# A four-layer graph network on one core: the second head's up-projection placed in steps around the first head's softmax

## The chip, the cores and the metric

One NeuronCore of one Trainium2 chip runs the kernel. The metric is the device time of one execution in microseconds (us), less is better. The engines are named by what they do here: TensorE (PE in the rows) multiplies, VectorE (DVE), ScalarE (ACT) and GpSimd (POOL) do the elementwise work, and SyncE (SP) issues most weight loads.

## What is computed

The input is `x` (256 nodes, 768 features) with 8192 edges (src, dst, and a type for layer 3). Four layers each add a graph part and a feed-forward part to `x`, each on a layer-normed input. The change touches layers 0 and 1, whose graph part is a two-stage graph attention:

```
def gat_conv(x, src, dst, W, a_src, a_dst, b, heads, out_ch):
    h = (x @ W).reshape(n, heads, out_ch)              # up-projection, 768 -> 8 heads x 768
    e = leaky_relu(alpha_src[src] + alpha_dst[dst], 0.2)
    p = exp(e - segment_max(e, dst)[dst])
    alpha = p / segment_sum(p, dst)[dst]
    out = segment_sum(h[src] * alpha, dst)             # attend
    return out.reshape(n, heads * out_ch) + b

h = elu(gat_conv(x, ..., W1, 8 heads, 768))            # 8 hidden heads
out = gat_conv(h, ..., W2, 1 head, 768)                # down-projection 8*768 -> 768, then attend again
```

Then come small feed-forward parts, a GCN layer (2) and a relational GCN layer with 34 relations (3), which the change leaves alone.

## The kernel before

The engines run programs of their own, ordered by hand and tied by semaphores; no planner is involved. All edges are first counted into dense 256x256 matrices (`cnt`), so that the segment softmax becomes a row softmax over a dense matrix weighted with the counts, and `attend` becomes a matmul with its transpose. The counting (`count`, 16 batches of 4 tiles of edges) shares the start of the kernel with head 0 of layer 0: VectorE and ScalarE make one-hot and ramp tiles in a ring of three, and TensorE takes them in between the steps of head 0's up-projection.

All weights stream through SBUF in chunks of 768x768 (six 128-row tiles, two parts of three). SP loads a part into `w_in` (`load`); ScalarE rounds it to the high half `w_hi` (`high`), and VectorE makes the rest `w_lo` (`low`). Each product of two values is three fp32r matmuls, high x high, high x low and low x high (`mm3`). Both `w_hi` and `w_lo` have two halves, so that one chunk is used while the next is made. `w_in` has one place for each part, so that a load waits until the part before it is rounded and its rest made.

A hidden head `h` is worked so, with one chunk of W1 and one of W2:

- TensorE: `up` (12 steps: 2 node tiles m times 6 tiles k, each two outputs of 384 columns, 6 matmuls), then `down(h - 1)` in three pieces (of its 12 steps 3, 6 and 3), with `spread(h)` (the source scores laid out as a row in bank 7) after 3 and `turn(h)` (the transpose of `alpha`) after 9, then `attend(h)` (36 matmuls of 256 columns, in three groups).
- ScalarE: keeps `h_sb` and `h_hi` from the banks (`keep_tile`), exponentials of the scores, `aT_hi`, then `z_b` (`kept`), the exponential for elu (`exponential`) and the rounding of `hid_hi` (`rounded`), and the high halves of two weight chunks in between.
- VectorE: four dot products for the scores (the third releases `spread`), softmax in `scores` to `alpha` (semaphore `normed`), a low part `ahead`, `aT_lo`, a second low part, then elu (`negative`, `unit`), `batch_firsts` (which edge of a cell is its first, for a table on layer 3's relations), `remainder` (`hid_lo`), and the low parts of the W2 chunk.

Head 0 has no `down` before it. Between its `spread`, `turn` and `attend` TensorE runs zero matmuls (`seed`, `idle`: 128x128 zeros with 512 columns), 3 of which also clear the sums in banks 0, 1 and 2. The heads 1 to 7 are one loop on TensorE; ScalarE and VectorE have head 0 and head 7 written out. The last head does the three elu stages interleaved, the others stage after stage. The chunk of a W1 sits in half `layer` of the weight buffers, that of a W2 in half `1 - layer`.

SP starts with the load of chunk 1, then waits until it has arrived, clears the 9 MB `table` in HBM, and goes on with the loads W1(1), W2(0), W1(2), W2(1) and so on. GpSimd adds the edges into that table with indirect DMAs.

`step_of`, `up`, `down`, `attend`, `spread`, `turn`, `seed` and `idle` are TensorE's functions; the helper line 435 records nearly all its matmuls, line 531 the transposes of `alpha`. ScalarE's helper `keep` is line 948, VectorE's `tt` is 1267 and `dot` 1273.

## Time and profile before

| | us |
|---|---|
| median of 3 runs | 1368.61 (1365.76 to 1372.85) |
| the profiled execution | 1376.49 |
| its span, first to last instruction | 1374.5 |
| TensorE matmuls busy | 1304.2 (95%) |
| VectorE busy | 994.7 (72%) |
| ScalarE busy | 646.9 (47%) |
| share of TensorE in the chain that ended last | 82% |
| mean granted TensorE clock | 0.98 |

A granted clock of 1.00 is 2.4 GHz, 0.50 is 1.2 GHz. Times in the rows are us from the span's start. A row of a timeline stands for one or several like instructions in a row; its second number runs from the first start to the last end.

### The profile page before, as it was taken

How to read it: one execution, taken by the hardware profiler on the slowest of the kernel's cores; microseconds unless marked ns; L12 is line 12 of the kernel's file. 1: busy time of each engine (PE TensorE's matmuls, PEld its weight loads, DVE VectorE, ACT ScalarE, POOL GpSimd, SP SyncE). 2: the span in 40 equal slices, each digit the busy share in tenths (PEclk: the TensorE clock that was granted, in tenths of full speed). 3: DMA queues.
4: the chain of work that ended last, by engine and by line, in shares of the span. 5: the costliest groups of instructions: out<-in, count | busy, mean ns of one | idle time of the engine just before them, and what ended most of it. 6: DMA issues, size and time to landing. Idle time of an engine off the chain costs nothing.

```text
span 1374.5 us, 21211 instructions
## 1 busy us (share of the span) xinstructions
PE 1304.2 (95%) x7822; PEld 1153.0 (84%) x7822; DVE 994.7 (72%) x1634; ACT 646.9 (47%) x845; POOL 215.7 (16%) x160
## 2 busy tenths in 40 slices
PE   6899999988899999988898999999999999999987
PEld 5699999965799999967777888988898888988876
DVE  7888888987688888876757666655666556665556
ACT  5666565554466565654334343333433344333342
POOL 0034443340034444440000000000000000002000
PEclk9999999999999999998989999999999999999989
DMA  9755665654355665635314644554445444553530
GB/s 306 262 177 168 179 212 181 196 130 136 107 175 168 197 205 175 193 92 178 108 60 167 223 153 154 188 190 154 153 164 192 178 153 153 177 194 117 179 91 28
DMA packets 103875, 227.33 MB, mean 165 GB/s; under 512 B 16710, under 2 KB 34950, under 8 KB 103840
## 3 DMA queue, kind: packets, MB, share of 16 engines
q1 hardware_dynamic: 72924, 192.43, 40.0%
q10 hardware_dynamic: 20980, 31.78, 8.2%
q0 software_dynamic: 9936, 2.66, 2.0%
q8 instruction: 21, 0.34, 0.1%
q14 instruction: 14, 0.11, 0.0%
HBM read 216.56 MB, written 10.29 MB: 165 GB/s over the span
## 4 chain that ended last, share of the span: by engine, by line
PE 82%; DVE 11%; ACT 2%; issue 2%; DMA 1%; ACTq 0%; DVEq 0%; SPq 0%
PE bank L435 81%; DVE w_lo L1267 3%; DVE stats L1305 1%; ACT w_hi L948 1%; PE bank L474 1%; DVE h_lo L1267 1%; PE bank L531 1%; DMA w_in<-L_gnn_W_root 1%; DVE xT_lo L1267 1%; DVE neg_b L1270 0%; DMA x_sb<-x 0%; DVE x_sb L1267 0%; DMA w_in<-L_gnn_W 0%; DVE scores_b L1273 0%; DVE hid_lo L1267 0%
## 5 line engine op out<-in xcount | busy, mean ns | idle before, releaser
L1267 DVE TENSOR_TENSOR w_lo<-w_in,w_hi 128x2304 fp32r<-128x2304 f32 (+4 forms) x162 | 396.5, 2477 | 60.7 <-ACT w_hi L948 60.6
L948 ACT ACTIVATE w_hi<-w_in 128x2304 fp32r<-128x2304 f32 (+4 forms) x162 | 328.1, 2062 | 224.3 <-PE bank L435 197.2
L435 PE MATMUL bank<-w_hi,xT_hi 128*128 128x384 f32 (+3 forms) x942 | 326.3, 346 | 4.7 <-DVE xT_lo L1267 3.4
L435 PE MATMUL bank<-w_lo,xT_hi 128*128 128x384 f32 (+3 forms) x942 | 309.8, 341 | 0.0
L435 PE MATMUL bank<-w_hi,hid_hi 128*128 128x512 f32 (+3 forms) x858 | 293.5, 342 | 5.0 <-DVE hid_lo L1267 4.8
L435 PE MATMUL bank<-w_lo,hid_hi 128*128 128x512 f32 (+3 forms) x858 | 271.7, 337 | 0.0
L435 PE MATMUL bank<-w_hi,xT_lo 128*128 128x384 f32 (+3 forms) x942 | 247.5, 341 | 0.0
L435 PE MATMUL bank<-w_hi,hid_lo 128*128 128x512 f32 (+3 forms) x858 | 224.9, 338 | 0.0
L435 PEld LDWEIGHTS bank<-w_hi,xT_hi 128*128 128x128 f32 (+1 forms) x942 | 178.9, 190 | 31.9 <-issue 6.2
L435 PEld LDWEIGHTS bank<-w_hi,hid_hi 128*128 128x128 f32 (+1 forms) x858 | 161.5, 188 | 41.2 <-issue 5.9
L435 PEld LDWEIGHTS bank<-w_lo,xT_hi 128*128 128x128 f32 (+1 forms) x942 | 179.0, 190 | 13.2
L1774 DVE SCALAR_TENSOR_TENSOR neg_b<-bank,rinv,neg_b 128x512 f32<-128x512 f32 (+1 forms) x136 | 77.5, 611 | 154.4 <-PE bank L435 154.4
L435 PEld LDWEIGHTS bank<-w_lo,hid_hi 128*128 128x128 f32 (+1 forms) x858 | 161.7, 188 | 18.4
L394 POOL DMA_INDIRECT table<-value,row_i x64 | 122.8, 1919 | 243.0 <-DMA table<-value,row_i 224.7
L435 PEld LDWEIGHTS bank<-w_hi,xT_lo 128*128 128x128 f32 (+1 forms) x942 | 157.9, 191 | 2.1
L435 PEld LDWEIGHTS bank<-w_hi,hid_lo 128*128 128x128 f32 (+1 forms) x858 | 134.5, 190 | 1.0
L435 PE MATMUL bank<-aT_hi,h_hi 128*128 128x256 f32 (+1 forms) x408 | 107.5, 283 | 2.2 <-DVE aT_lo L1267 2.2
L435 PE MATMUL bank<-aT_hi,h_lo 128*128 128x256 f32 (+1 forms) x408 | 107.6, 286 | 0.0
L948 ACT ACTIVATE xT_hi<-bank 128x512 fp32r<-128x512 f32 (+1 forms) x87 | 46.8, 554 | 124.9 <-PE bank L435 63.5
L435 PE MATMUL bank<-aT_lo,h_hi 128*128 128x256 f32 x396 | 104.8, 283 | 0.0
L420 POOL DMA_INDIRECT w_in<-L_gnn_W_rel,xrow_i x6 | 7.3, 1216 | 527.1 <-DVE w_lo L1267 525.6
L435 PEld LDWEIGHTS bank<-aT_hi,h_hi 128*128 128x128 f32 x408 | 78.3, 192 | 5.0 <-DVE aT_lo L1267 3.6
(252 smaller groups left out, 1566.2 us busy)
## 6 DMA issues: line engine op xcount, KB each, us to landing
w_in<-L_gnn_W_rel SPq DMA_DIRECT2D x68, 1152.0 KB, 5.9
w_in<-L_gnn_W SPq DMA_DIRECT2D x66, 1152.0 KB, 6.2
table<-zrow SPq DMA_DIRECT2D x1, 9216.0 KB, 31.6
scores_b<-table ACTq DMA_DIRECT2D x34, 256.0 KB, 3.0
a_bc<-L_gnn_a_src ACTq DMA_DIRECT2D x18, 384.0 KB, 3.8
a_bc<-L_gnn_a_dst ACTq DMA_DIRECT2D x18, 384.0 KB, 5.3
key_row<-key_rows ACTq DMA_DIRECT2D x16, 256.0 KB, 5.4
w_in<-ffn_out SPq DMA_DIRECT2D x4, 864.0 KB, 7.3
```

Of the source, the lines that this page charges most:

```text
L394: pool.indirect_dma_start(out=cells, out_offset=bass.IndirectOffsetOnAxis(ap=row_i[:, g:g + 1], axis=0), in_=value[:, g:g + 1], in_offset= ...
L420: pool.indirect_dma_start(out=w_in[:, p, k, :], out_offset=None, in_=t["L3_gnn_W_rel"], in_offset=bass.IndirectOffsetOnAxis(ap=xrow_i[:, 3 ...
L435: return pe.matmul(out, lhsT, rhs, start=start, stop=stop, **kw)
L474: last = pe.transpose(bank[TURNED[i][m][half]][:, k * P:(k + 1) * P], xn[:, m, (3 * half + k) * P:(3 * half + k + 1) * P], ident[:, :])
L531: last = pe.transpose(bank[7][:, sm * N + m * P:sm * N + (m + 1) * P], alpha[:, m, sm * P:(sm + 1) * P], ident[:, :])
L948: act.activation(out, ps, func, **kw).then_inc(mark, 1)
L1267: return dve.tensor_tensor(out, a, b, op)
L1305: last = dve.bn_stats(stats[:, m, j, :], x_sb[:, m, j * HALF:(j + 1) * HALF])
L1774: last = dve.scalar_tensor_tensor(xs, bank[b][:, c0:c1], weight, xs, mul, add_)
```

## The change

Head 1's up-projection leaves the loop. Its 12 steps are laid around head 0's softmax in layer 0 as 0 before `spread`, 6 before `turn`, none before `attend` and 6 after it, and in layer 1 as 2, 6, 1 and 3. The zero matmuls there go, but for 3 and 3 short fillers in layer 0 and the three that clear the sums, which now stand behind the up-projection. So that the steps have their banks, head 0 attends into banks 0, 1, 2. Chunk 2 of a layer is loaded next to chunk 1 (in layer 0 ahead of the clearing) and split early. The chunks alternate between the two halves in both layers alike. Head 0 does elu interleaved, `second_count` stands behind `alpha`, and layer 1's bias is added after head 7.

```diff
@@ SP
                 load(n0 + 1, w1[:, 0:D])
+                load(n0 + 2, w1[:, D:2 * D])
                 if layer == 0:
                     sp.wait_ge(zeroed, 1)
-                    for p in range(2):
-                        sp.wait_ge(w_full[p], 16)
                     sp.dma_start(table.rearrange("(p t) n -> p t n", p=P),
...
-                with sp.Fori(0, HEADS - 1) as h:
-                    load(h * 2 + (n0 + 2), w1[:, bass.ds((h + 1) * D, D)])
+                with sp.Fori(0, HEADS - 2) as h:
                     load(h * 2 + (n0 + 3), w2[bass.ds(h * D, D), :])
+                    load(h * 2 + (n0 + 4), w1[:, bass.ds((h + 2) * D, D)])
+                load(n0 + 2 * HEADS - 1, w2[(HEADS - 2) * D:(HEADS - 1) * D, :])
@@ TensorE
+                def up_second(steps):
+                    for m, k in steps:
+                        if k == 0:
+                            pe.wait_ge(h_high, 9 * layer * 4 + 2 * m + 2)
+                        if k == 3:
+                            pe.wait_ge(w_low[1], n0 + 3)
+                        last = step_of(m, UP_BANKS[m], k, n0 + 2, 1)
+                        if k == K - 1:
+                            last.then_inc(*((h_mm, 1) if m == 0 else (w_used, 1)))
...
-                up(0, n0 + 1, True)
-
-                spread(9 * layer)
-                if layer == 0:
-                    pe.wait_ge(e_mask, 1)
-                    pe.wait_ge(e_kept, 2)
-                seed((0, 1, 2))
-                seed((0,) * 22)
-                turn(9 * layer)
-                seed((0,) * 5)
-                parts_kept(9 * layer)
-                attend(0)
-                with pe.Fori(1, HEADS) as h:
-                    up(h, h * 2 + n0)
+                def rest_of(h):
                     down(h - 1, h * 2 + (n0 + 1), 0, 3)
                     spread(h + 9 * layer)
                     down(h - 1, h * 2 + (n0 + 1), 3, 9)
                     turn(h + 9 * layer)
                     down(h - 1, h * 2 + (n0 + 1), 9, M * K)
                     parts_kept(h + 9 * layer)
-                    attend(h)
+                    attend()
+
+                if layer == 0:
+                    second = [(m, k) for k0 in (0, 3) for m in range(M) for k in range(k0, k0 + 3)]
+                else:
+                    second = [(m, k) for m in range(M) for k in range(K)]
+                before_spread, before_turn, before_sum = ((0, 6, 6), (2, 8, 9))[layer]
+
+                up_first()
+                up_second(second[:before_spread])
+                spread(9 * layer)
+                if layer == 0:
+                    idle(6, 3)
+                up_second(second[before_spread:before_turn])
+                turn(9 * layer)
+                up_second(second[before_turn:before_sum])
+                if layer == 0:
+                    idle(2, 3)
+                parts_kept(9 * layer)
+                if layer == 0:
+                    pe.wait_ge(e_mask, 1)
+                    pe.wait_ge(e_kept, 2)
+                attend((0, 1, 2))
+                up_second(second[before_sum:])
+                pe.wait_ge(z_kept, 3 * HEADS * layer + 3)
+                seed((0, 1, 2))
+                rest_of(1)
+                with pe.Fori(2, HEADS) as h:
+                    up(h, h * 2 + n0)
+                    rest_of(h)
@@ ScalarE
-                    high(h * 2 + (n0 + 2), h * 2 + (c0 + 3), layer, parts=(0,))
+                    if not first_head:
+                        high(h * 2 + (n0 + 2), h * 2 + (c0 + 3), 1, parts=(0,))
                     attend(u, ahead)
-                    high(h * 2 + (n0 + 2), h * 2 + (c0 + 3), layer, parts=(1,))
+                    if not first_head:
+                        high(h * 2 + (n0 + 2), h * 2 + (c0 + 3), 1, parts=(1,))
+                    elif layer == 0:
+                        high(n0 + 2, 1, 1, parts=(1,))
...
-                    if last_head:
+                    if first_head or last_head:
...
+                if b == 7:
+                    high(2, 1, 1, parts=(0,))
...
             tile_by_tile(2)
+            high(NTH_GAT[1] + 2, used(C_GAT[1] - 1), 1)
             gat(1, lambda: None)
@@ VectorE
-                    scores(h + 9 * layer, layer, lambda: low(h * 2 + (n0 + 2), layer, parts=(0,)),
-                           begun=first_head and layer == 0, meanwhile=second_count if first_head and layer == 0 else lambda: None)
-                    low(h * 2 + (n0 + 2), layer, parts=(1,))
+                    if first_head:
+                        ahead = second_count if layer == 0 else lambda: None
+                    else:
+                        def ahead():
+                            low(h * 2 + (n0 + 2), 1, parts=(0,))
+
+                    scores(h + 9 * layer, layer, ahead, begun=first_head and layer == 0)
+                    if not first_head or layer == 0:
+                        low(h * 2 + (n0 + 2), 1, parts=(1,))
...
+                if layer == 1:
+                    low(n0 + 2, 1)
                 head(0, first_head=True)
...
                 low_chunk(c0 + 18)
-                if layer == 0:
-                    biased(0)
+                biased(layer)
...
+                if b == 11:
+                    low(2, 1, parts=(0,))
...
-            boundary(2, ffn0_out, 1)
+            boundary(2, ffn0_out)
```

## Rows read from the trace of the kernel before

**Rows 1.** Chain that ended last: start, length, engine, tile, helper line, count

```profile
60.85 29.27 PE bank L435 x166
```

**Rows 2.** TensorE's timeline, layer 0: start, length, line, operation, [idle before, released by]

```profile
48.91 5.57 PE L435 MATMUL bank<-zero 128*128 128x512 bf16 x25 [0.29 <-DVE rdeg L1518]
57.78 0.66 PE L531 MATMUL bank<-ident,alpha 128*128 128x128 f32 x4 [3.31 <-DVE alpha L1270]
...
60.85 0.58 PE L435 MATMUL bank<-aT_hi,h_hi 128*128 128x256 f32 x1 [0.85 <-DVE aT_lo L1267]
...
67.40 0.33 PE L435 MATMUL bank<-w_hi,xT_hi 128*128 128x384 f32 x1
...
79.90 0.39 PE L435 MATMUL bank<-w_hi,hid_hi 128*128 128x512 f32 x1
...
83.09 0.71 PE L435 MATMUL bank<-ident,scal 128*128 128x128 f32 x4
```

**Rows 3.** Stretches: length, busy us of PE, PEld, DVE, ACT, POOL; granted clock, DMA, GB/s

```profile
61.00:65.00 4.00, 4.00 (x19) 4.00 (x20) 2.87 (x2) 0.93 (x3) 0.00 (x0) 0.50 0.66 233
...
373.00:377.00 4.00, 4.00 (x31) 4.00 (x30) 2.01 (x5) 2.81 (x7) 0.00 (x0) 1.00 0.95 339
```

**Rows 4.** VectorE's timeline, layer 0: the counting, then head 0's softmax

```profile
41.55 0.30 DVE L1267 TENSOR_TENSOR spare<-iota,edge_f 128x136 bf16<-128x136 bf16 x1 [0.77 <-PE bank L435]
...
54.70 0.68 DVE L1267 TENSOR_TENSOR cnt<-spare 128x512 f32<-128x512 f32 x1
...
56.10 0.42 DVE L1273 CUSTOM_DVE_ANT_0 scores_b<-prob,cnt 128x256 f32<-128x256 f32 x1
...
57.65 2.55 DVE L1267 TENSOR_TENSOR w_lo<-w_in,w_hi 128x2304 fp32r<-128x2304 f32 x1
60.11 0.68 DVE L1267 TENSOR_TENSOR aT_lo<-bank,aT_hi 128x512 fp32r<-128x512 f32 x1
```

**Rows 5.** Timelines of ScalarE and VectorE: a head of the loop, then head 7

```profile
98.06 0.84 ACT L1020 ACTIVATE z_b<-bank,b_head 128x256 f32<-128x256 f32 x2 [0.60 <-PE bank L435]
...
105.05 5.02 DVE L1267 TENSOR_TENSOR w_lo<-w_in,w_hi 128x2304 fp32r<-128x2304 f32 x2
...
112.57 0.96 DVE L1273 CUSTOM_DVE_ANT_0 spare<-z_b,a_bc 128x768 f32<-128x768 f32 x1 [0.16 <-DVE scal L1273]
...
280.87 0.84 ACT L1020 ACTIVATE z_b<-bank,b_head 128x256 f32<-128x256 f32 x2
...
287.42 3.82 DVE L1267 TENSOR_TENSOR w_lo<-w_in,w_hi 128x1728 fp32r<-128x1728 f32 x2
```

**Rows 6.** TensorE's timeline, layer 1, head 0

```profile
360.72 0.71 PE L435 MATMUL bank<-ident,scal 128*128 128x128 f32 x4 [2.10 <-DVE scal L1273]
...
367.55 0.66 PE L531 MATMUL bank<-ident,alpha 128*128 128x128 f32 x4 [0.73 <-DVE alpha L1270]
...
370.62 0.39 PE L435 MATMUL bank<-aT_hi,h_hi 128*128 128x256 f32 x1 [1.33 <-DVE aT_lo L1267]
...
375.04 0.33 PE L435 MATMUL bank<-w_hi,xT_hi 128*128 128x384 f32 x1
```

**Rows 7.** Timelines of ScalarE and VectorE, layer 1, head 0

```profile
349.98 0.87 ACT L948 ACTIVATE xT_hi<-bank 128x384 fp32r<-128x384 f32 x2 [5.05 <-PE bank L474]
...
368.74 2.12 ACT L948 ACTIVATE w_hi<-w_in 128x2304 fp32r<-128x2304 f32 x1
...
359.70 0.96 DVE L1273 CUSTOM_DVE_ANT_0 spare<-z_b,a_bc 128x768 f32<-128x768 f32 x1 [3.77 <-ACT z_b L948]
```

**Rows 8.** DMA issues: out<-in, engine, operation, count, KB each, us to landing

```profile
w_in<-L_gnn_W SPq DMA_DIRECT2D x66, 1152.0 KB, 6.2
table<-zrow SPq DMA_DIRECT2D x1, 9216.0 KB, 31.6
```

**Rows 9.** Timelines: GpSimd's first edge batch, and VectorE after head 7 of layer 1

```profile
72.95 0.56 POOL L382 TENSOR_TENSOR value<-first,ones 128x4 f32<-128x4 f32 x1 [24.05 <-DVE again L1270]
...
602.69 0.96 DVE L1273 CUSTOM_DVE_ANT_0 spare<-z_b,a_bc 128x768 f32<-128x768 f32 x1 [3.56 <-ACT z_b L948]
```

More of the change, by code:

```diff
@@ L539, in gat, with step_of @@
                 c0, n0, b0 = C_GAT[layer], NTH_GAT[layer], layer * HEADS
-                def up(h, n, first=False):
-                    def step_of(m, banks, k):
-                        if m == 0 and k % 3 == 0:
-                            pe.wait_ge(w_low[k // 3], n + 1)
-                        if first:
-                            of_tile(2 * layer, m)(k)
-                        return mm3([(bank[banks[j]][:, 0:HALF], part(w_hi, w_lo, slice(0, P), layer, k, slice(j * HALF, (j + 1) * HALF)))
-                                    for j in range(2)],
-                                   part(xT_hi, xT_lo, slice(0, P), k, slice(m * P, (m + 1) * P)), k == 0, k == K - 1)
-                    if first and between is not None:
-                        between(step_of)
+                def step_of(m, banks, k, n, half, first=False):
+                    if m == 0 and k % 3 == 0:
+                        pe.wait_ge(w_low[k // 3], n + 1)
+                    if first:
+                        of_tile(2 * layer, m)(k)
+                    return mm3([(bank[banks[j]][:, 0:HALF], part(w_hi, w_lo, slice(0, P), half, k, slice(j * HALF, (j + 1) * HALF)))
+                                for j in range(2)],
+                               part(xT_hi, xT_lo, slice(0, P), k, slice(m * P, (m + 1) * P)), k == 0, k == K - 1)
@@ L555, in up, with up_first @@
+                def up_first():
+                    if between is not None:
+                        between(lambda m, banks, k: step_of(m, banks, k, n0 + 1, 0, True))
                         return
[L556 to L559 removed]
+                    for m in range(M):
                         for k in range(K):
[L561 to L562 removed]
+                            last = step_of(m, UP_BANKS[m], k, n0 + 1, 0, True)
+                        last.then_inc(*((h_mm, 1) if m == 0 else (w_used, 2)))
@@ L1363, in tile_low, with scores @@
                 low_of(h_lo[:, m, :], h_sb[:, m, :], h_hi[:, m, :], h_low)
-            def scores(u, layer, ahead, together=False, begun=False, meanwhile=lambda: None):
+            def scores(u, layer, ahead, together=False, begun=False):
                 if not begun:
@@ L1448, in head @@
                             remainder(j)
-                        low(h * 2 + (n0 + 3), 1 - layer)
+                    if not last_head:
+                        low(h * 2 + (n0 + 3), 0)
+                if layer == 1:
+                    low(n0 + 2, 1)
                 head(0, first_head=True)
```

53 lines of the change are left out of this document (28 added, 25 removed).

## The prediction

> **What bounds the kernel now.** I read the chain of waits first. Through a hidden layer's heads it is one unbroken stretch of TensorE work, 29.27 us for the first turn of the loop alone [rows 1], so TensorE's order of work is the bound there. The chain leaves TensorE only at the seams. The change touches two of them: the softmax of head 0 in layer 0 (about 48 to 67 us) and in layer 1 (about 360 to 375 us). So I read TensorE's timeline there next, then VectorE's and ScalarE's over the same time.
>
> At both seams TensorE has nothing useful to do. In layer 0 it runs 25 zero matmuls (5.57 us, 0.223 us each), stands for 3.31 us until VectorE has `alpha`, turns it, runs 5 more, stands 0.85 us for `aT_lo`, and then attends from 60.85 to 67.40: 6.55 us for 36 matmuls [rows 2]. In layer 1 the same 36 take 4.42 us (370.62 to 375.04), after idle times of 2.10, 0.73 and 1.33 us [rows 6]. The difference of 2.1 us is the clock: granted 0.50 (1.2 GHz) between 61 and 65 us, 1.00 (2.4 GHz) between 373 and 377 us [rows 3]. Then comes head 1's up-projection, 12 steps in 12.50 us (67.40 to 79.90), so 1.04 us a step, and 3 steps of the down-projection, 3.19 us, up to the spread of head 1's scores at 83.09 [rows 2].
>
> The question is what ends last at that spread. It needs VectorE's third dot product. In the loop that dot is at 112.57 to 113.53, after weights (105.05), a copy and two more dots; the last `z_b` pair, which is released by the end of attend, starts at 98.06 [rows 5]. So VectorE's way from attend's end to the spread is 113.5 - 98.06 = 15.5 us, and TensorE's own (12 up steps and 3 down steps) is 12.50 + 3.19 = 15.7 us. They are level. That decides what the change is worth: taking up steps out from between attend(0) and spread(1) frees TensorE, and the spread is then set by VectorE.
>
> **The change part by part, layer 0.** The sum is made against the profiled execution's own 1376.49 us (span 1374.5 us), 0.6% above the median of 1368.61 us; a gain of a few us is carried over as it is.
>
> (a) VectorE now makes the first half of chunk 2's low part after batch 11 of the edge counting. It costs 2.47 us (half of 5.02, [rows 5]) and falls on an idle time of 0.77 us before the next batch [rows 4]. From there on VectorE goes from batch to batch without a pause, so the counts end and head 0's last dots start about 1.65 us later. ScalarE's matching half (2.12 us, [rows 7]) comes at batch 7, where it still waits for TensorE at every later batch; I cost it at nothing, and without that cover it would be 2.1 us.
>
> (b) `second_count` goes from ahead of the sums of the exponentials to behind `alpha`. Those sums start at 56.10, and the count began at 54.70 [rows 4]; the exponentials are there by then, so they start 1.35 us earlier. `alpha` comes at 57.75 + 1.65 - 1.35, about 58.0.
>
> (c) Behind `alpha` VectorE made a 2.55 us low part at 57.65, and `aT_lo` waited behind it until 60.11 [rows 4]. Now the 1.35 us count stands there, and `aT_hi` comes out later than its end: `aT_lo` starts at about 59.35. TensorE: the spread at about 49.7, 3 zero matmuls (0.67 us), 6 steps (6.25 us) to 57.0, 1.0 us of standing, turn at 58.0, 3 zero matmuls, attend from 60.0. It stood 3.31 us before and now stands twice for under 1.1 us, so I take the clock as full: 4.4 us, end at 64.4 against 67.40. That is 3.0 us, of which 2.1 are the clock.
>
> (d) After attend: 6 steps to 70.7, three zero matmuls to 71.3, then the down-projection, which waits for the low part of chunk 3. Its place on VectorE: head 0 now has the last head's interleaved order. In that order the weights' low part starts 287.42 - 280.87 = 6.55 us after the last `z_b` pair begins, in the loop's order 105.05 - 98.06 = 6.99 us [rows 5]. Only 0.44 us is gained, since the work on VectorE is the same. In layer 0 the second half of chunk 2 (2.47 us) ends at about 63.9 now, in the midst of attend, and takes that back. So low part 3 starts at 71.3, its first half is done at 73.8 (TensorE stands 2.5 us), 3 steps end at 77.0, and the third dot at 71.3 + 8.5 = 79.8: TensorE stands another 2.8 us. The spread comes at 79.9 against 83.09: 3.2 us gained. The 27 zero matmuls dropped (6.0 us, against 6 new ones, 1.3 us) and the 6 steps moved up have turned mostly into these two waits. From there on both engines are level as before, so the lead stays to the end.
>
> **Layer 1.** (e) Both halves of the second chunk are now made ahead of head 0's scores. ScalarE is free at 350.85 [rows 7], makes 2 x 2.12 us to 355.1 and then keeps tile 0; VectorE follows from 353.0 with 2 x 2.47 us to 358.0, where it had the bias (1.8 us, now gone to after head 7) and then idled 3.77 us before the third dot at 359.70 [rows 7]. The first two dots (2 us) now come after it, so the third starts at about 360.25: 0.55 us late. TensorE uses the 2.10 us before the spread for two steps, and 6 more behind it (6.25 us, to 367.9), just in time for `alpha` at 368.0.
> (f) No low part stands ahead of `aT_lo` any more. It can start 1.35 us after turn begins, at 369.4; attend starts at 370.0 against 370.62 and ends at 374.4: 0.6 us gained.
> (g) After it TensorE has only 3 up steps and 3 zero matmuls, to 378.2. Low part 3 starts at 374.4 + 6.55 = 381.0, its half is there at 383.5: TensorE stands 5.3 us. The third dot ends at 381.0 + 8.5 = 389.5. Before it was 375.04 + 15.7 = 390.7: 1.2 us gained.
>
> **The rest.** The bias of layer 1 after head 7 falls into an idle time of 3.56 us on VectorE [rows 9]: nothing; without it, 1.8 us. SP's order: the load of chunk 2 goes ahead of the clearing of the table. This load waits until chunk 1 is split (about 22 us), so the clearing starts some 8 us later and takes 31.6 us, and a load takes 6.2 us [rows 8]. Chunk 2 is then there by 30 us, well before batch 7's use, and the clearing ends at about 54; its first real user on POOL starts at 72.95 after idling 24.05 us for VectorE [rows 9]. Nothing, and beyond 24 us of delay it would count. Chunk 3's second half loads from 63.9 to 70.1 and is needed at 71. The swap of the buffer halves costs nothing, as no instruction is added. What an unrolled head costs at the joint no row shows: from 0 to the 0.85 us of the second idle time in rows 2, and I take 0, nearest to the unbroken stretch of rows 1.
>
> **The clock** is the unknown term. New standing times are 2.5 and 2.8 us in layer 0, 5.3 and about 1 us in layer 1. The row with 3.31 us idle was followed by 1.2 GHz [rows 2, 3], the one with 2.10 us was not [rows 3, 6]. 2.8 us lies between. At half clock TensorE has half the output: a stretch like that of rows 3 (some 4 to 7 us) costs 2 to 3.4 us where TensorE is the bound, and nothing where it waits anyway, as before spread(1). After layer 1's long gap most of the slow time falls under the remaining wait; after the one of 2.8 us it falls on the path. I take 1.0 us for both, between 0 and 6.8.
> By the Trainium skill (TensorE: Matmul & The Clock Gate, Part 1: The HAM clock gate) the half rate is the default, activity lifts it, and the check runs free of the kernel, so that equal gaps can end differently. By that rule the 2.8 us gap would drop the clock in some executions and not in others; the trace agrees in so far as 3.31 us and 2.10 us went apart.
>
> Sum: -3.2 - 1.2 + 1.0 = -3.4 us, so 1373.1 us for the profiled execution and 1365.2 us for the median.
>
> **Rivals.**
> A. The forecast, 1363 to 1367.5: 52%.
> B. Slower: the new waits cool the clock. Both spreads of head 1 are followed by 1.2 GHz as long as in rows 3, 3.4 us each: 6.8 - 4.4 = +2.4, 1371.0 us. It decides from a stretch of about 2.2 us lost in each layer. For it: 3.31 us sufficed once, and the new gaps come in pairs. Against: layer 1's 2.10 + 0.73 + 1.33 us left the clock full [rows 3, 6]. 16%.
> C. The gain is given back at once: VectorE's added 1.65 us in the counting and the clock of attend not regained (2.1 us), so layer 0 gives 1.1 and layer 1 0.5 us less the clock's 1.0: 1368.0 us. For it: two standing times still lie around turn. 16%.
> D. The spread follows TensorE, as it would if VectorE's 15.5 us were mostly waits for head 1's `h_sb`. Then layer 0 gains 3.0 + 6.25 and layer 1 0.6 + 9.4 less the zero matmuls, 18 us: 1350. Against it stands rows 5: from 105.05 on VectorE goes through without a wait. A part of it (some us) is likelier than the whole: 16%, mostly at 1358 to 1362.
>
> Range: 1360 to 1371 leaves out the far ends of B and D. About 0.5% (6.8 us) is what can be told from no change: faster by more (under 1361.8) 18%, slower by more 5%, within it 77%.
>
> **What would show it.** Right: attend(0) of layer 0 takes 4.4 us at a granted clock of 1.00 and ends some 3 us earlier; the standing before the down-projection's first step is put down to `w_lo`, and before head 1's spread to `scal`, in both layers, longest in layer 1; the counting ends some 1.6 us later; from head 2 on each turn takes what it took, and the lead neither grows nor shrinks. Wrong: no standing before spread(1) (then D), a granted clock of 0.50 behind it (B), or attend(0) still above 6 us (C). A stand for `w_hi` or for the load of chunk 3 in layer 0 would mean that the clearing's new place costs, which I have at nothing.

## The result, and the profile after

The changed kernel is slower by a few us. The median of 6 runs is 1375.75 us (1373.64 to 1377.65), against 1369.37 us for 6 runs of the kernel before on the same chip: a ratio of 1.0043 (95% interval 1.0023 to 1.0063). Two later sets of 12 runs of the same kernel gave 1.0023 (1.0007 to 1.0040) and 1.0015 (0.9997 to 1.0033). So the loss is 2 to 6 us, and the mean of the three ratios gives 3.7 us. Forecast were 1365.2 us and a range of 1360 to 1371: wrong in sign, and outside the range.

The profiled execution took 1374.94 us, its span 1372.5 us. That is less than the profiled execution before (1376.49), although the medians go the other way. That execution before was 7 us above its own median, and this needed a look of its own (e0_before).

| | before | after |
|---|---|---|
| median on the same chip, us | 1369.37 | 1375.75 |
| profiled execution / span, us | 1376.49 / 1374.5 | 1374.94 / 1372.5 |
| TensorE matmuls busy, us | 1304.2 | 1294.1 |
| TensorE in the chain that ended last | 82% | 79% |
| mean granted clock | 0.98 | 0.979 |

TensorE does 10 us less, since the zero matmuls are gone, and none of it has come off the end. The chain of waits says where it stays. In the profile after it leaves TensorE in the seam of layer 0, where it ran through before [rows 1]. Columns: start, length, what held the chain.

```profile
58.04 0.67 PE bank L532 x4
...
61.37 2.57 DVE w_lo L1309
...
64.15 9.34 DMA w_in<-L_gnn_W
73.51 2.14 ACT w_hi L981
...
76.00 2.15 issue
...
81.73 9.42 PE bank L436 x40
91.59 30.04 PE bank L436 x184
```

A weight load of 9.34 us is on the path, from 64.15 to 73.5. The forecast had it landed at 70.1. TensorE's timeline of layer 0, answering to [rows 2]:

```profile
58.04 0.66 PE L532 MATMUL bank<-ident,alpha 128*128 128x128 f32 x4 [1.03 <-DVE alpha L1312]
...
60.17 0.38 PE L436 MATMUL bank<-aT_hi,h_hi 128*128 128x256 f32 x1 [0.83 <-DVE aT_lo L1309]
...
70.87 0.82 PE L436 MATMUL bank<-zero 128*128 128x512 bf16 x3
...
74.08 0.47 PE L436 MATMUL bank<-w_hi,hid_hi 128*128 128x512 f32 x1 [2.39 <-DVE w_lo L1309]
...
81.73 1.22 PE L436 MATMUL bank<-ident,scal 128*128 128x128 f32 x4 [4.26 <-DVE scal L1315]
```

Up to 77 us this is the forecast line by line: turn at 58.0, attend from 60.2, a stand of 2.39 us for `w_lo` (forecast 2.5). Then comes a stand of 4.26 us for `scal` where 2.8 was forecast, and the spread of head 1 at 81.73 instead of 79.9. ScalarE and VectorE in that time:

```profile
68.69 2.12 ACT L981 ACTIVATE w_hi<-w_in 128x2304 fp32r<-128x2304 f32 x1
73.51 2.13 ACT L981 ACTIVATE w_hi<-w_in 128x2304 fp32r<-128x2304 f32 x1 [2.71 <-DMA w_in<-L_gnn_W]
```

```profile
71.39 2.55 DVE L1309 TENSOR_TENSOR w_lo<-w_in,w_hi 128x2304 fp32r<-128x2304 f32 x1
75.67 2.56 DVE L1309 TENSOR_TENSOR w_lo<-w_in,w_hi 128x2304 fp32r<-128x2304 f32 x1 [1.74 <-ACT w_hi L981]
```

ScalarE waits 2.71 us for the second half of chunk 3, VectorE 1.74 us for ScalarE, and the dots behind it shift by that: 79.9 + 1.7 = 81.6.

The stretches, columns as in [rows 3] (length; busy PE, PEld, DVE, ACT, POOL; granted clock, DMA share, GB/s):

```profile
64.00:67.00 3.00, 3.00 (x21) 3.00 (x20) 2.55 (x6) 2.88 (x7) 0.00 (x0) 1.00 0.95 33
81.00:85.00 4.00, 3.27 (x11) 2.98 (x12) 3.90 (x8) 1.40 (x1) 0.00 (x0) 0.50 0.64 231
85.00:89.00 4.00, 4.00 (x19) 3.41 (x19) 3.90 (x11) 0.91 (x2) 1.56 (x1) 0.75 0.43 111
...
385.00:389.00 4.00, 2.50 (x8) 2.16 (x9) 3.90 (x3) 3.26 (x9) 3.87 (x2) 0.50 0.32 48
```

They show two things. From 64 to 67 us the DMA engines are busy (0.95) but move 33 GB/s; the stretch of [rows 3] at a share of 0.95 moved 339. And right behind the spread the granted clock is 0.50 to 0.75, so that the way from head 1's spread to head 2's takes 32.88 us (81.73 to 114.61); before it took 30.50 (83.09 to 113.59). The changed kernel is 1.4 us ahead at the spread of head 1 and 1.0 us behind at that of head 2.

Layer 1, answering to [rows 6]:

```profile
363.72 0.71 PE L436 MATMUL bank<-ident,scal 128*128 128x128 f32 x4 [0.43 <-DVE scal L1315]
...
370.57 0.66 PE L532 MATMUL bank<-ident,alpha 128*128 128x128 f32 x4
...
372.64 0.39 PE L436 MATMUL bank<-aT_hi,h_hi 128*128 128x256 f32 x1 [0.35 <-DVE aT_lo L1309]
...
386.50 0.77 PE L436 MATMUL bank<-w_hi,hid_hi 128*128 128x512 f32 x1 [5.47 <-DVE w_lo L1309]
...
392.33 0.71 PE L436 MATMUL bank<-ident,scal 128*128 128x128 f32 x4 [0.49 <-DVE scal L1315]
```

The stand of 5.47 us (forecast 5.3) is there. From spread(0) to spread(1) it takes 28.61 us, before 30.02.

### The profile page after: what moved, and what is told of

The parts are those of the page before. It is cut to its first block, busy times and chain, and to the rows that moved or that the text cites. A ratio compares the mean times of both kernels' runs of the same rounds, so it can differ in the third digit from the quotient of the medians.

```text
span 1372.5 us, 21078 instructions
## 1 busy us (share of the span) xinstructions
PE 1294.1 (94%) x7774; PEld 1147.2 (84%) x7774; DVE 995.4 (73%) x1634; ACT 646.1 (47%) x845; POOL 215.5 (16%) x160
## 4 chain that ended last, share of the span: by engine, by line
PE 79%; DVE 12%; issue 3%; ACT 3%; DMA 2%; DVEq 0%; ACTq 0%; SPq 0%
PE bank L436 78%; DVE w_lo L1309 3%; ACT w_hi L981 1%; DMA w_in<-L_gnn_W 1%; DVE stats L1347 1%; PE bank L475 1%; PE bank L532 1%; DMA w_in<-L_gnn_W_root 1%; DVE h_lo L1309 1%; DVE xT_lo L1309 1%; DVE neg_b L1312 0%; DMA x_sb<-x 0%; DVE x_sb L1309 0%; DVE hid_lo L1309 0%; DVE neg_b L1549 0%
## 5 line engine op out<-in xcount | busy, mean ns | idle before, releaser
L981 ACT ACTIVATE xT_hi<-bank 128x512 fp32r<-128x512 f32 (+1 forms) x87 | 46.7, 553 | 124.8 <-PE bank L436 63.4
L1309 DVE TENSOR_TENSOR xT_lo<-bank,xT_hi 128x512 fp32r<-128x512 f32 (+1 forms) x87 | 52.9, 631 | 39.2 <-ACT xT_hi L981 38.6
```

The source lines that it names most:

```text
L981: act.activation(out, ps, func, **kw).then_inc(mark, 1)
L1309: return dve.tensor_tensor(out, a, b, op)
```

## The experiments

Each is timed against the kernel before on the same chip; the ratio is followed by its 95% interval. All but the repeats are edits of the changed kernel. Executions of one kernel lie 3 to 7 us either side of their median, and behind the last of the points below one execution needs 943 to 953 us, so that a step of 1 or 2 us can't be read from whole times. It is read from the traces, at these points (us from the span's start; L0 and L1 are the layers, s0 to s2 the spreads of heads 0 to 2):

| kernel | ratio | L0 s0 | L0 s1 | L0 s2 | L1 s0 | L1 s2 |
|---|---|---|---|---|---|---|
| before | | 48.01 | 83.09 | 113.59 | 360.72 | 421.29 |
| e0_before | 0.9988 | 47.84 | 81.07 | 111.55 | 359.51 | 420.12 |
| after | 1.0043 | 49.48 | 81.73 | 114.61 | 363.72 | 422.92 |
| e4_after | 1.0023 | 49.36 | 85.09 | 117.64 | 365.04 | 424.20 |
| e14_after | 1.0015 | 49.58 | 83.42 | 115.87 | 365.10 | 424.33 |
| e1_fill | 0.9998 | 49.48 | 82.62 | 113.09 | 361.35 | 420.50 |
| e2_firsts | 0.9996 | 49.57 | 82.26 | 114.27 | 361.55 | 420.17 |
| e3_l1old | 1.0008 | 49.59 | 82.45 | 114.44 | 362.50 | 423.11 |
| e7_l0old | 0.9981 | 49.42 | 82.35 | 112.84 | 361.04 | 420.28 |
| e8_latedump | 0.9990 | 49.50 | 79.86 | 110.34 | 359.14 | 418.31 |
| e9_three | 0.9991 | 49.28 | 81.21 | 111.74 | 360.00 | 418.62 |
| e11_split | 0.9986 | 50.16 | 80.57 | 111.04 | 359.04 | 418.37 |
| e12_both | 0.9995 | 49.42 | 81.25 | 111.91 | 361.02 | 420.18 |
| e13_l0old_late | 0.9988 | 49.67 | 81.07 | 111.48 | 360.32 | 419.88 |

**e0_before, e4_after, e14_after: the same kernels again.**

> The kernel before, unchanged, for a second profiled execution and for the ratio that no change gives. The profiled execution of before took 1376.49 us, 7 us more than the median of its timed runs (1369.4), while that of the changed kernel (1374.94) is at its own median (1375.75). Theory 1 (the change costs what its trace shows at the seams, and the profiled execution of before had lost some 7 us elsewhere that most executions don't lose, in stretches at 1.2 GHz): ratio 1.000, a profiled execution near 1369 us with fewer stretches at 1.2 GHz than in the first. Theory 2 (timed executions differ from profiled ones in general): again a profile some 7 us above the median.

0.9988 (0.9971 to 1.0004), so two builds of one kernel agree within 0.12%. The profiled execution took 1370.24 us, its own median, so a profiled execution is not slower as such. The second profile shows what was particular in the first. TensorE in it:

```profile
57.62 0.89 PE L531 MATMUL bank<-ident,alpha 128*128 128x128 f32 x4 [3.31 <-DVE alpha L1270]
...
65.38 0.33 PE L435 MATMUL bank<-w_hi,xT_hi 128*128 128x384 f32 x1
...
81.07 0.71 PE L435 MATMUL bank<-ident,scal 128*128 128x128 f32 x4
```

The same stand of 3.31 us as in [rows 2], but the granted clock is back at 0.96 from 61 to 65 us where it was 0.50 [rows 3]. Attend ends at 65.38 and not at 67.40, and the spread comes at 81.07 and not at 83.09. Two of the 3.2 us that I forecast for layer 0 were in that one profile and not in this one.

> The changed kernel again, unchanged, on the chip of the next three, for their comparison and for a second profile. Theory 1: 3 to 6 us slower than before (ratio 1.002 to 1.004); in the trace the second loop turn's spread in layer 0 comes at 114.6 us as in the first profile (before: 113.6 and 111.6 in its two profiles), and in layer 1 the stretch from the first transpose of the normed input to head 2's spread takes 77 to 78.5 us (before: 77.9).

> The changed kernel a third time, beside the two above, for their difference: ratio to before 1.002 to 1.004; chunk 3's second half lands at 73.5 us or later and 1.2 GHz is granted right behind the wait for it.

1.0023 (1.0007 to 1.0040) and 1.0015 (0.9997 to 1.0033). The spread of head 1 is at 85.09 and 83.42, later than in the first profile after, and in both the load is late again. In e4_after ScalarE waits for it for 6.25 us:

```profile
76.88 2.12 ACT L981 ACTIVATE w_hi<-w_in 128x2304 fp32r<-128x2304 f32 x1 [6.25 <-DMA w_in<-L_gnn_W]
```

**e1_fill: zero matmuls in the new standing times.**

```
 rest_of(1):
+    for _ in range((10, 24)[layer]): mm(bank[1], zero, zero)     # ahead of the first 3 steps of down
     down(...)
+    for _ in range((18, 4)[layer]): mm(bank[1], zero, zero)      # ahead of spread(1)
```

> The changed kernel with zero matmuls (0.223 us each) added in the two new standing times before head 1's spread: 10 and 18 in layer 0, 24 and 4 in layer 1. They should fit into waits of 2.39 and 4.26 us and of 5.47 and 0.49 us. Theory 1 (each of the new standing times is followed by a stretch at 1.2 GHz, which costs TensorE some 2.4 us behind the spread in layer 0 and about 1 in layer 1): 3 to 4 us faster than the changed kernel, about 1372 us, granted clock 1.00 from 60 to 100 us and from 372 to 400. Theory 2 (the loss lies elsewhere, such as in loads, and the slow stretches fall into waits): no change, 1375.5 us, though the clock is full.

0.9998 (0.9982 to 1.0014). TensorE, then the stretch behind the spread:

```profile
77.24 4.06 PE L436 MATMUL bank<-zero 128*128 128x512 bf16 x18
82.62 0.71 PE L436 MATMUL bank<-ident,scal 128*128 128x128 f32 x4 [1.31 <-DVE scal L1322]
```

```profile
81.00:85.00 4.00, 2.69 (x17) 2.17 (x16) 3.77 (x9) 1.04 (x1) 1.86 (x1) 1.00 0.84 275
```

The clock stays at 1.00, and the way from s1 to s2 is 30.47 us instead of 32.88. The load is late again (landed at 74.4). So the clock costs 2.4 us and is one of two causes.

**e2_firsts: head 0's `batch_firsts` ahead of elu instead of behind it.**

```
     scores(...)
+    if first_head: batch_firsts(b)
     ...
     remainder(2)
-    batch_firsts(b)
+    if last_head: batch_firsts(b)
```

> The changed kernel with VectorE's batch_firsts of head 0 (1.95 us) taken from between hid_lo and the low part of chunk 3 and put behind aT_lo, where VectorE idles 1.25 us in layer 0 and 2.66 us in layer 1. If VectorE's chain sets head 1's spread, the spread comes 1.2 us earlier in layer 0 (less where the late load of chunk 3 caps it: then 0) and 1.5 to 2 us earlier in layer 1, so 2 to 3 us faster in all, about 1373 us. If the spread followed TensorE or a load, the time stays at 1375.5 us.

0.9996 (0.9979 to 1.0012). In layer 1 the way s0 to s2 is 58.62 us instead of 59.20: 0.6 us gained where I had expected 1.5 to 2; why not more stays open. In layer 0 nothing: VectorE is earlier, but the second half's load still is not there (landed at 74.0).

**e3_l1old and e7_l0old: the 12 steps back behind attend, in layer 1 alone and in layer 0 alone.** The weights' halves, SP's order and VectorE's order stay as changed.

```
-before_spread, before_turn, before_sum = ((0, 6, 6), (2, 8, 9))[layer]
+before_spread, before_turn, before_sum = ((0, 6, 6), (0, 0, 0))[layer]   # e3_l1old
+before_spread, before_turn, before_sum = ((0, 0, 0), (2, 8, 9))[layer]   # e7_l0old
+    in that layer: idle(6, 25) before turn, idle(6, 5) behind it
```

> The changed kernel, but in layer 1 the 12 steps of head 1's up-projection all stand behind attend again, with zero matmuls (25 and 5) around turn as before; the early split of the second chunk, the banks and the elu order stay. VectorE's chain to head 1's spread is not touched, so if it is what ends last there, the spread comes at the same time and only the slow stretch behind the 5.5 us gap goes: 0 to 1.5 us faster than the changed kernel, 1374.5 us. If layer 1's placement gains what it was laid out for (8 steps moved off the path, 8 us), this is 8 us slower, 1383 us. If it is the placement in layer 1 that costs most of the measured 6 us, it is 4 us or more faster, 1371 us.

1.0008 (0.9988 to 1.0028). The way s0 to s2 of layer 1 is 60.61 us, as before (60.57, and 60.61 in e0_before). With the steps moved it is 59.15 to 59.24 in after, e1_fill, e4_after, e14_after, e7_l0old, e8_latedump and e12_both (59.33 in e11_split, 59.56 in e13_l0old_late). The steps are worth 1.4 us there: neither nothing, as if VectorE alone set that spread, nor the 8 us of the steps' own length.

> The changed kernel, but in layer 0 the 12 steps of head 1's up-projection all stand behind attend again, with zero matmuls around turn (28 and 8); the counting's low part, the loads' order, the banks and the elu order stay. Theory 1: head 1's spread stays at about 82 us, since VectorE and the late half of chunk 3 set it, TensorE has no standing time left before it and keeps 2.4 GHz behind it: 1.5 to 2.5 us faster than the changed kernel, head 2's spread at about 112.5. If the placement of the steps gains anything in layer 0, this is slower than the changed kernel, by up to 6 us.

0.9981 (0.9963 to 0.9999), the lowest ratio of all, and by medians 6.8 us under e4_after of the same set. With the steps behind attend, TensorE hardly stands ahead of the spread:

```profile
82.35 0.71 PE L436 MATMUL bank<-ident,scal 128*128 128x128 f32 x4 [1.39 <-DVE scal L1319]
```

The way from s1 to s2 is 30.49 us, at full clock. The load is late in it too (landed at 74.1), and so the spread is at 82.35. So the steps' place in layer 0, by the stand it makes, and not VectorE's new order, brings the low clock.

**e5_clear and e6_all: the clearing back at its early time, on ScalarE's queue.** The suspicion: the clearing (9 MB, now 8 us later) disturbs chunk 3's load.

```
-sp.dma_start(table, zrow)                    # behind the load of chunk 2
+act.wait_ge(zeroed, 1); act.dma_start(table, zrow)      # behind load_heads(0, 0)
```

> The changed kernel, but the clearing of the table is issued by ScalarE's queue right after the first heads' vectors (about 15 us), so that it runs beside the load of chunk 2 and not behind it on SP's queue. In four profiles of kernels with the change the second half of chunk 3 landed at 73.5 to 74.4 us, 9.3 to 10.3 us after its issue (median of such loads 5.9), and the low part and the spread of head 1 waited for it. Theory 1a (its lateness comes from the clearing's new place, which ends some 10 us later than before): it lands by 70.5, the spread comes at 80 instead of 81.7 to 82.5, 1.5 to 2.5 us faster than the changed kernel. Theory 1b (a load issued at this point is late for another reason, such as the first read of a new weight tensor): it lands at 73.5 again and nothing changes. Risk: chunk 2 lands late under the clearing and ScalarE's batch 8 waits; then slower.

> The changed kernel with three edits together: the clearing on ScalarE's queue, batch_firsts of head 0 behind aT_lo, and zero matmuls in the remaining standing times (1 and 12 in layer 0, 15 and 12 in layer 1). Theory 1 (late load, VectorE's chain and the slow stretches add up): layer 0 reaches head 2's spread at about 110.5 us, layer 1's stretch takes about 76 us, and the time is 5 to 7 us below the changed kernel and 2 to 3 us below before (ratio 0.998). If the causes overlap, it equals before (1.000).

1.0187 (1.0163 to 1.0211) and 1.0188 (1.0165 to 1.0211): 27 and 25 us slower, where I had expected some us less. ScalarE's queue and ScalarE itself:

```profile
18.21 27.44 ACTq L1119 DMA_DIRECT2D key_rows<-key_t  x1
45.77 4.89 ACT L1126 ACTIVATE spare<-iota,edge_f 128x256 bf16<-128x256 bf16 x12 [27.59 <-issue]
```

The DMA behind the clearing on the same queue is 32 KB, and issuing it took 27.44 us (0.54 us in the changed kernel, where the clearing is on SP's queue); ScalarE stood as long, and TensorE 23.29 us for ScalarE. SP's queue is held up too. In the kernel before, the first load of chunk 2 stands behind the clearing, and its issue, begun at 19.75, took 20.79 us. SP's load issues of the first 60 us there (shortest, median and longest in ns, first and last start):

```profile
L301 SPq DMA_DIRECT2D w_in<-L_gnn_W x4: 434/900/20788, 2.9 to 40.8; - x4
```

In e5_clear, with the clearing off SP's queue, the same load was issued at 19.50 in 0.37 us. The hold cost the kernel before next to nothing: ScalarE waited 0.81 us for that chunk at 49.49, TensorE not at all. As an answer to the question the two say one thing only. With the clearing long done, chunk 3 loads on time, and from s0 to s1 e5_clear needs 30.37 us. The forecast has 79.9 - 49.7 = 30.2 us for that.

**e8_latedump: GpSimd's first indirect addition later.** The traces' records of the single packets led to it. Between the clearing and its real work GpSimd issues one indirect addition of zeros (128 elements) into `table`. It waits for the clearing only. GpSimd's row of it, and that of the view of DMA issues (count, us from issue to landing):

```profile
57.39 1.76 POOL L407 DMA_INDIRECT table<-zrow,dump_i  x1 [53.47 <-DMA table<-zrow]
```

```profile
table<-zrow,dump_i POOLq DMA_INDIRECT x1, 10.0
```

Before it was issued at 46.88. The clearing is 8 us later now, so it is 10.5 us later. Its packets of 4 B are through at 62.4 us, and that I took for its landing in the expectation below. But it counts as landed only at 67.4, so the load issued at 64.15 runs beside it. In the eight profiles where an addition issued at 57 to 59 us does this, the first 32 packets of the load take 1.4 to 2.4 us each on average (single ones up to 3.6 us in this profile and 6.6 us in e4_after), where others take 0.12. This is the stretch of 33 GB/s. The edit moves the addition alone:

```
 pool.wait_ge(cleared, 16)
+pool.wait_ge(b_first, 1)       # batch_firsts of head 0, which its real work needs anyway
 pool.indirect_dma(table <- zrow, dump_i, add)
```

> The changed kernel, but GpSimd's first indirect DMA, which adds zeros to 128 spare rows of the table, also waits for VectorE's first batch_firsts (about 71 us) and not for the clearing alone (57 us). In all profiles of the change it lands at about 62 us, the load of chunk 3's second half is issued at 64.1 us, and its first 32 or so packets then take 1.3 to 2.6 us each instead of 0.12; the half lands at 73.5 to 76.9. In before the same addition landed at 53 us and the vectors loaded at 56 had slow packets too (0.5 to 1.3 us). Theory A (the indirect addition slows what is read right behind it): the half lands by 70.5, head 1's spread comes at 80 us, 2 to 4 us faster than the changed kernel. Theory B (the 9 MB of writes of the clearing, ended at 54 to 57 us, do it): the packets stay slow, the half lands at 73.5 or later, no change.

0.9990 (0.9969 to 1.0010). GpSimd, ScalarE, TensorE and the stretch:

```profile
72.39 3.13 POOL L408 DMA_INDIRECT table<-zrow,dump_i  x1 [68.47 <-DVE again L1313]
```

```profile
68.65 4.12 ACT L982 ACTIVATE w_hi<-w_in 128x2304 fp32r<-128x2304 f32 x2
```

```profile
74.04 0.47 PE L437 MATMUL bank<-w_hi,hid_hi 128*128 128x512 f32 x1 [2.38 <-DVE w_lo L1310]
...
79.86 0.71 PE L437 MATMUL bank<-ident,scal 128*128 128x128 f32 x4 [0.89 <-DVE scal L1316]
```

```profile
64.00:67.00 3.00, 3.00 (x20) 3.00 (x20) 2.57 (x6) 2.90 (x7) 0.00 (x0) 1.00 0.54 148
81.00:85.00 4.00, 4.00 (x25) 3.51 (x24) 3.93 (x7) 1.82 (x3) 0.00 (x0) 1.00 1.01 115
```

ScalarE makes both halves without a wait. The first 32 packets take 0.3 us on average, and the same 3 us move 148 GB/s. The spread is at 79.86; 79.9 was forecast. Its stand is short, the clock behind it is 1.00, and s2 is at 110.34. The clearing's place is unchanged in this kernel, which refutes that its writes delay the load. The addition's place caused the late load, and the late load made the long stand.

**e9_three: e8_latedump, e2_firsts and fills of (1, 13) and (15, 12) zero matmuls together.**

> The changed kernel with the late first addition of the run before, batch_firsts of head 0 behind aT_lo, and zero matmuls in the standing times left (1 and 13 in layer 0, 15 and 12 in layer 1). If theory A holds: head 1's spread at 78 us, head 2's at 108.8, layer 1's stretch to head 2's spread 76 us, ratio to before 0.996. If theory B holds, the load caps layer 0: head 2's spread at 112.5 to 113, ratio 0.998 to 0.999.

0.9991 (0.9970 to 1.0012), and the spread at 81.21, worse than e8_latedump alone. The two edits interact: `b_first` is now released early, so the addition goes out before the load again, and the load is late again. GpSimd, then ScalarE, then the stretch before ScalarE's row:

```profile
62.77 3.13 POOL L408 DMA_INDIRECT table<-zrow,dump_i  x1 [58.85 <-DVE again L1320]
...
74.71 0.20 POOL L383 TENSOR_TENSOR value<-first,ones 128x4 f32<-128x4 f32 x1 [8.81 <-DMA table<-zrow,dump_i]
```

```profile
72.99 2.13 ACT L989 ACTIVATE w_hi<-w_in 128x2304 fp32r<-128x2304 f32 x1 [1.85 <-DMA w_in<-L_gnn_W]
```

```profile
70.30:72.90 2.60, 1.51 (x8) 0.62 (x6) 1.73 (x1) 0.84 (x1) 0.00 (x0) 1.00 0.00 0
```

A failure as an attempt at the best kernel, and a second sign of the cause: this time the addition was moved to the load, with the clearing unchanged. The delay has another form here. The first 32 packets of the load take 0.32 us on average, much as in e8_latedump, and the last is through at 70.2; yet from there to the landing at 73.0 the DMA engines move nothing. GpSimd's next row, at 74.71, waited for the addition, which confirms that it was under way all that time.

**e10_l0old_more: e7_l0old with e2_firsts and fills (0, 0) and (15, 12).**

> Layer 0 with all 12 steps behind attend (as in the kernel that was the fastest so far, ratio 0.998), layer 1 with the change's placement, batch_firsts of head 0 behind aT_lo in both, and zero matmuls in layer 1's standing times (15 and 12). Layer 0: head 2's spread at about 112 us, since the late load still caps VectorE. Layer 1: the stretch takes 76 us instead of 77.9 (before). Ratio to before 0.997 to 0.998. If batch_firsts' place gains nothing, 0.998 to 0.999.

0.9998 (0.9978 to 1.0019), nothing over e7_l0old. Its spreads in layer 0 are at 82.45 and 112.92. In layer 1 it misses what I expected: the way s0 to s2 is 60.18 us, though e9_three needs 58.62 with the same edits there. Its granted clock is 0.68 from 385 to 389 us, in the steps ahead of the spread, so zero matmuls in a stand did not keep the clock full every time.

**e11_split: the clearing in two halves around chunk 2's load.** This moves the addition earlier.

```
+clear(0)
 load(n0 + 2, ...)
-clear
+clear(1)            # GpSimd waits for both
```

> The changed kernel, but the clearing goes in two halves: the first as soon as chunk 1 has landed (14.3 us, as in before), then chunk 2, then the second half. The DMA engines have no idle time between 14 and 20 us, and the clearing and the indirect addition behind it end some 4 us earlier. Under both theories on the late load the distance to it grows, so chunk 3's second half lands by 70.5 to 72, head 1's spread comes at 80 to 81, 1 to 2.5 us faster than the changed kernel. Against it: chunk 2's first half lands only at about 33 us instead of 26, just where ScalarE wants it (32.5); if it comes 4 us later than that, the counting waits and it is slower.

0.9986 (0.9966 to 1.0006). The addition goes out at 51.95 and lands at 61.1, 3.7 us ahead of the load's issue at 64.80. The load is on time, and TensorE has the spread at 80.57:

```profile
80.57 0.71 PE L444 MATMUL bank<-ident,scal 128*128 128x128 f32 x4 [0.90 <-DVE scal L1323]
```

From s0 to s1 it needs 30.41 us, e8_latedump 30.36. So an addition moved the other way works as well, though here half of the clearing moved with it.

**e12_both: e8_latedump and zero matmuls (10, 11) and (24, 11).**

> The changed kernel with both causes taken away: GpSimd's first addition waits for batch_firsts (so the load of chunk 3 is on time) and zero matmuls fill the standing times before the down-projection and before head 1's spread (10 and 11 in layer 0, 24 and 11 in layer 1). If late load and slow stretches are the whole loss and add up, what is left is what was forecast without its clock term: head 2's spread in layer 0 at 110.3 us (before 111.6 and 113.6), layer 1's stretch 76.9 us (before 77.9), 3 us below before, ratio 0.998, and some 6 us below the changed kernel run beside it. If they overlap (a timely load leaves too short a wait to cool the clock), it equals the kernel with the late addition alone, 0.999.

0.9995 (0.9981 to 1.0010). Way s1 to s2: 30.66 us. This execution had a granted clock of 0.57 from 60 to 64 us, in attend itself, so s1 came at 81.25. Of the time with both causes away it says no more than that it is near that of the kernel before.

**e13_l0old_late: e7_l0old and e8_latedump.**

> Layer 0 with all 12 steps behind attend, plus GpSimd's late first addition. VectorE sets head 1's spread, so with a timely load it comes at 79.9 us, TensorE standing for nothing: head 2's spread at 110.3 as with the change's placement, ratio 0.998. If TensorE's 12 steps behind attend set it instead (64.5 + 12.5 + 0.7 + 3.2 = 80.9), 1.0 us later, ratio 0.9985; that 1.0 us is then all that the placement of the steps is worth in layer 0.

0.9988 (0.9973 to 1.0003). Here the load is on time and the steps stand behind attend. TensorE comes to the spread without standing:

```profile
81.07 0.61 PE L437 MATMUL bank<-ident,scal 128*128 128x128 f32 x4
```

So s1 is set by TensorE at 81.07, and with the steps moved by VectorE at 79.86 (e8_latedump). At s2 it is 111.48 against 110.34. That is what the placement in layer 0 is worth by itself: 1.1 us.

**The addition and the load in the profiles** (us from issue to landing of each; the load is that of chunk 3's second half):

| kernel | addition | load | took |
|---|---|---|---|
| before | 46.9 to 59.4 | 63.9 to 70.7 | 6.8 |
| e0_before | 46.7 to 58.6 | 64.0 to 69.7 | 5.7 |
| e11_split | 52.0 to 61.1 | 64.8 to 71.2 | 6.4 |
| e8_latedump | from 72.4 | 64.1 to 70.5 | 6.4 |
| e12_both | from 73.8 | 64.0 to 69.4 | 5.3 |
| after | 57.4 to 67.4 | 64.2 to 73.5 | 9.3 |
| e1_fill | 58.3 to 67.2 | 64.1 to 74.4 | 10.3 |
| e2_firsts | 59.0 to 69.1 | 64.8 to 74.0 | 9.2 |
| e3_l1old | 58.8 to 68.0 | 64.2 to 74.2 | 10.0 |
| e4_after | 58.7 to 69.8 | 64.0 to 76.9 | 12.9 |
| e7_l0old | 58.7 to 68.7 | 64.0 to 74.1 | 10.1 |
| e9_three | 62.8 to 74.6 | 64.5 to 73.0 | 8.5 |
| e10_l0old_more | 58.8 to 68.3 | 64.6 to 74.2 | 9.6 |
| e14_after | 58.9 to 69.8 | 64.2 to 75.2 | 11.0 |

In every profile where the addition is still under way when the load is issued, the load takes 8.5 us or more; in every other one it takes 6.8 us or less. The profile of e13_l0old_late (addition from 72.6) gives no landing, but ScalarE goes through both halves without a wait there.

## Why the prediction was wrong, step by step

**(a), (b), (c) right in their times, but (c) took its gain from a slow base.** Turn at 58.04 (forecast 58.0), attend from 60.17 (60.0), its end at 64.4 to 64.7 (forecast 64.4) in ten of the thirteen profiles of changed kernels without e5_clear and e6_all. e11_split has 65.24, with the counting 0.7 us later, and e12_both and e14_after have 65.97 and 66.13, with a granted clock of 0.57 from 60 to 64 us. The base was particular: e0_before has 65.38, so that against it 0.7 to 1.0 us is gained at full clock and not 3.0. The 2.1 us between the two clocks of [rows 3] belonged to single executions, on both sides, and I took them for a property of the kernel before. That step of the forecast was wrong too.

**(d) failed, by one clause of "The rest".** The placement and VectorE's length were right: e8_latedump has the stand of 2.38 us (forecast 2.5) and the spread at 79.86. What failed is "Chunk 3's second half loads from 63.9 to 70.1 and is needed at 71", with the clearing's new place put at nothing. It was issued at 64.15 and landed at 73.5 in the first profile, 75.2 and 76.9 in the repeats: 9.3 to 12.9 us instead of the median of 6.2 [rows 8]. It had 0.9 us to spare. I had weighed the later clearing only against GpSimd's first real user at 72.95 [rows 9] and missed the indirect addition at 46.88 that waits for nothing but the clearing. The row itself held the hint: an idle time of 24.05 us ahead of 72.95 begins at 48.90, so GpSimd had done something until then (46.88 + 2.02). Price: the spread at 81.7 to 85.1 instead of 79.9.

**(e), (f), (g) right.** From the start of layer 1's head 0 to its spread it takes 17.74 to 17.78 us in ten changed kernels (before 17.34 and 17.32): 0.4 us late, forecast 0.55. The first profile after has 19.31 there, e12_both 19.33 and e10_l0old_more 19.36: they ran at 0.57 and 0.64 from 346 to 350 us (after, e10_l0old_more) and at 0.59 from 343 to 347 (e12_both); why there I cannot say. From s0 to s2 1.4 us are gained. Net 1.0 us, forecast 1.2. The stand was 5.47 us, forecast 5.3.

**The clock term was too small, and in one place.** I took 1.0 us for both layers. In layer 1 it is next to nothing in the changed kernel, as argued: after has 59.20 us from s0 to s2, e1_fill with the gap filled and the clock full 59.15. (It can cost more there: e10_l0old_more lost 1.6 us against e9_three.) In layer 0 it is 1.5 to 2.4 us: from s1 to s2 the five profiles with a late load and a long stand (after, e4_after, e14_after, e2_firsts, e3_l1old) need 31.99 to 32.88 us, e1_fill and e8_latedump 30.47 and 30.48. The stand there was not the forecast 2.8 us but 3.42 to 7.80, because of the load; with e8_latedump's 0.89 us no clock was lost behind the spread (it was 0.62 from 74 to 78 us, behind the stand of 2.38 us, where the rest of the wait covered it). So the second error came for the most part out of the first.
By the Trainium skill (TensorE: Matmul & The Clock Gate, Part 1: The HAM clock gate) a check that runs free of the kernel lets equal gaps end differently. The trace agrees: after the same stand of 3.31 us attend took 6.55 us in one execution of the kernel before and ended 2.02 us earlier in the other.

**The rest right in what it covered.** The bias, the swap of halves and the unrolled head cost nothing that a trace shows: e13_l0old_late, which has them all, is at 0.9988, and the bias leaves VectorE 1.78 us of idle time behind head 7 in the profile after.

**Rivals.** B was nearest with its 1371.0 us and had the right kind of event, but only behind one of its two spreads, and not from the new gaps as such. C fell in most executions: attend ran at full clock in 4.4 us, except in two of thirteen profiles. D fell: e13_l0old_late and e8_latedump lie 1.2 us apart at s1, since VectorE's way and TensorE's are level, as the first part says.

**The sum.** At s2 of layer 0 the two profiles before stand at 111.55 and 113.59, mean 112.6; the three of the changed kernel at 114.61, 117.64 and 115.87, mean 116.0: 3.5 us lost. Layer 1 gives back 1.0 us. That makes +2.5 us, in the lower part of the 2 to 6 us measured. From the forecast of -3.4 us it is 5.9 us away, and the terms give them: 3.5 us for the load (s1 at 83.4 on average instead of 79.9), 1.2 us for the clock behind it (s1 to s2 32.6 us on average against 30.5 in e8_latedump, so 2.2 us instead of 1.0), 1.0 us because the profile that the sum started from had the slower attend (its s2 is 1.0 us above the mean of the two before), and 0.2 us in layer 1.
Without the late load and the clock loss e8_latedump is 3.2 us ahead of the first profile before at s1, as forecast, but only 1.2 us ahead of e0_before, there and at s2. Its lead over e0_before is 1.8 us at the last point of the table, and its whole span is 1.8 us longer: what follows that point hides such a gain in a single execution. Its ratio of 0.9990 can't be told from 1, and of all versions only e7_l0old lies just outside its interval (0.9981, up to 0.9999). With this many kernels timed I don't call it a gain.

**Open.** Why the load took 9.3 us once and 12.9 us once beside the same addition; what in the addition holds the load up, and why at its first packets in eight profiles and at its end in e9_three; and why the ratio of one kernel was 1.0043 in the first set and 1.0015 in the last. e12_both was to show whether the two causes add up, and its one profile is disturbed in attend, so that is argued from e1_fill and e8_latedump and not shown by one kernel.

## What to carry to other kernels

When a DMA is moved, follow everything that waits for its semaphore, not the first user that computes with it: here a dummy addition of 128 elements was carried along by 10.5 us, into a load that had 0.9 us to spare. Take a DMA as under way until it has landed, not until its packets are through. Where two engines are level at a seam, work moved off one of them turns into standing time, and every stand ahead of the bound engine's next long stretch is a risk for the clock, so that the gain has to be larger than that risk. Profile the kernel before twice before taking a difference of clock as something to win.

## What the runs showed that I had not expected

- An indirect addition of 128 elements takes 8.9 to 13.7 us from issue to landing, although its packets are written within about 1.5 us, and a plain load issued while it is under way is late: 8.5 to 12.9 us to land in nine profiles, 5.3 to 6.8 us in the five others with a landing in the profile. In eight of the nine the first 32 packets of the load took 1.4 to 2.4 us each on average instead of 0.12.
- One DMA that clears 9 MB holds up the queue of the engine that issues it. On ScalarE's queue the next issue took 27.44 us and stood the engine as long, which cost the kernel 25 to 27 us (e5_clear, e6_all). On SP's queue the issue of the load behind it took 20.79 us in the kernel before (0.37 us with the clearing elsewhere), for which ScalarE waited only 0.81 us later on.
- A stand of 3.31 us was followed by 1.2 GHz for most of attend in one execution and by a granted clock of 0.96 from 61 to 65 us in the next of the same kernel: 2.0 us of difference at the next spread.
